# A fused decoder layer: order of instructions at the step from self- to cross-attention, and of the split of the output weights

## What is computed

```python
x = layernorm(x + self_attention(x))            # 32 heads of 16, causal
x = layernorm(x + cross_attention(x, context))  # 32 query heads of 128, 8 key/value heads, rotary positions
x = layernorm(x + experts(x))                   # 16 experts, 4 a token, and a shared one

# cross_attention
q = rope(x @ wq); k = rope(context @ wk); v = context @ wv
w = softmax(where(mask, q @ k.T / sqrt(128), -1e9))    # 4 query heads share a key head
out = (w @ v) @ wo
```

## Time and profile before

| | before |
|---|---|
| median of 3 runs | 1813.35 us (1811.98 to 1816.03) |
| profiled execution, its time | 1817.68 us |
| its span in the profile | 1815.9 us |
| TensorE busy | 1716.0 us (94%) |
| DVE busy | 1332.3 us (73%) |
| ScalarE busy | 925.3 us (51%) |
| GpSimd busy | 895.6 us (49%) |
| granted TensorE clock, mean | 0.978 of 2.4 GHz |

### The profile page before, as it was taken

The page is one execution under the profiler, slowest core; times in us unless marked ns, Lnnn a source line. Parts: engine busy times, 40 slices in busy tenths (PEclk is TensorE's granted clock), DMA queues, the critical chain, the costliest instruction groups (busy, mean ns, idle before and its releaser), DMA issues. The chain is left out here.

```text
span 1815.9 us, 39047 instructions
## 1 busy us (share of the span) xinstructions
PE 1716.0 (94%) x15412; PEld 991.1 (55%) x15412; DVE 1332.3 (73%) x2260; ACT 925.3 (51%) x1548; POOL 895.6 (49%) x732
## 2 busy tenths in 40 slices
PE   6999999899999999999999999999898999999990
PEld 4767676555555555555555555555454555455550
DVE  5788789688888888888888888888888444344445
ACT  4565657665646464556455555556631333333335
POOL 6643022564646454646455555556442455455551
PEclk9999999899999999999999999999999999999995
DMA  9610020211413222214122131212135678787668
GB/s 249 173 45 23 8 62 3 94 65 42 140 42 117 69 78 92 89 51 136 63 78 92 38 105 59 72 69 71 65 124 164 157 151 217 199 223 155 116 105 295
DMA packets 84946, 190.41 MB, mean 105 GB/s; under 512 B 10848, under 2 KB 29664, under 8 KB 82720
## 3 DMA queue, kind: packets, MB, share of 16 engines
q1 hardware_dynamic: 61680, 129.55, 21.2%
q0 software_dynamic: 23088, 58.37, 15.9%
HBM read 124.68 MB, written 63.21 MB: 103 GB/s over the span
## 5 line engine op out<-in xcount | busy, mean ns | idle before, releaser
L288 PE MATMUL bank<-xhl,front_h 128*128 128x512 f16 x704 | 267.5, 380 | 15.1 <-DVEq L68 13.5
L289 PE MATMUL bank<-xhl,front_h 128*128 128x512 f16 x704 | 267.6, 380 | 0.0
L290 PE MATMUL bank<-xhl,front_l 128*128 128x512 f16 x704 | 267.5, 380 | 0.0
L1004 POOL TENSOR_TENSOR xa_xs<-xa_xs,sn 128x512 f32<-128x512 f32 x160 | 233.9, 1462 | 45.7 <-ACT xa_xs L1056 45.7
L1015 POOL TENSOR_TENSOR xa_sc<-xa_sc,xa_rs 128x1024 f32<-128x1024 f32 x32 | 62.3, 1946 | 376.4 <-DVE xa_rs L1255 376.4
L1009 POOL TENSOR_TENSOR xa_rr<-xa_x,xa_xs 128x512 f32<-128x512 f32 x160 | 231.9, 1449 | 12.7 <-DVE xa_x L1160 0.2
L288 PE MATMUL bank<-out_h,xa_oh 128*128 128x512 f16 x512 | 194.9, 381 | 8.8 <-DVE xa_ol L1142 6.7
L1903 POOL DMA_INDIRECT scratch_y<-raw_front,moe_to x79 | 125.2, 1585 | 150.6 <-DVE mo_zl L1956 109.1
L289 PE MATMUL bank<-out_l,xa_oh 128*128 128x512 f16 x512 | 194.7, 380 | 0.0
L290 PE MATMUL bank<-out_h,xa_ol 128*128 128x512 f16 x512 | 194.6, 380 | 0.0
L1055 ACT ACTIVATE xa_xs<-bank 64x512 f32<-64x512 f32 x160 | 95.3, 595 | 131.2 <-PE bank L290 127.6
(11 more groups left out here) (299 smaller groups left out, 4756.5 us busy)
## 6 DMA issues: line engine op xcount, KB each, us to landing
xa_rawc<-in_ew SPq DMA_DIRECT2D x32, 768.0 KB, 5.6
moe_ring<-scratch_w SPq DMA_DIRECT2D x16, 1536.0 KB, 8.8
scratch_w<-xa_chunk_h SPq DMA_DIRECT2D x32, 384.0 KB, 2.3
scratch_w<-xa_chunk_l SPq DMA_DIRECT2D x32, 384.0 KB, 3.3
raw_front<-in_xwq SPq DMA_DIRECT2D x8, 1024.0 KB, 7.7
raw_out<-in_xwo SPq DMA_DIRECT2D x8, 1024.0 KB, 5.4
scratch_y<-xa_zero SPq DMA_DIRECT2D x18, 256.0 KB, 5.9
acc<-in_x POOLq DMA_DIRECT2D x4, 1024.0 KB, 12.9
```

What stands on the lines that cost most here:

```text
L288: pe.matmul(out_ap, ah, bh, start=start and m == 0, stop=False)
L289: pe.matmul(out_ap, ah, bl, start=False, stop=False)
L290: mm = pe.matmul(out_ap, al, bh, start=False, stop=stop and m == n - 1)
L1004: PO.mark(pool.tensor_tensor(xr, xr, sn[:, :].rearrange("p (a s) -> p a s", a=1) .to_broadcast([P, QT // S, S]), ALU.mult), f"sm{r}", st)
```

## The change

1. Self-attention, last group and quarter: DVE makes sums 0 and 1 behind sb3, not behind mx2, and counts them on a semaphore of their own (`s_late`); TensorE turns p2 and p3 ahead of rows 0 and 1.
2. Cross-attention, step (0, 0): TensorE makes the keys r0 of step (0, 1) between s0 and s1, into bank 1; r1 of (0, 1) goes to bank 6, and r3 of (0, 1) waits for cm0, which frees bank 1.
3. Step (0, 0): the four high halves of the tokens of quarter 1 stand ahead of h4 on ScalarE; two low halves ahead of l4 and two behind it on DVE, instead of behind sb1.
4. In all steps q = 1: woh stands behind pe1 on ScalarE, wol behind pl1 on DVE.

```diff
@@ -70,7 +70,7 @@
         for n in (name, *also):
-            key = n if step.i is None else (step.q, n)
+            key = n if step.i is None or isinstance(n, tuple) else (step.q, n)
             assert order[self.cursor] == key, (order[self.cursor], key)
@@ -330,6 +330,7 @@
                 s_st = [sem(f"sa_first{h}") for h in range(2)]
+                s_late = sem("sa_late_sums")
                 s_acc = [sem(f"sa_rows{n}") for n in range(NQ)]
@@ -631,10 +632,15 @@

-                    def most(st, j):
+                    def late_add(st, t):
+                        dve.wait_ge(PE.sem, PE.value(f"w{t}", st))
+                        row = acc[:, t + TQ * (st.q - 1), :]
+                        dve.scalar_tensor_tensor(row, home[f"w{t}"][:, :], 1 / (WS * WS), row, ALU.mult, ALU.add).then_inc(s_late, 1)
+
+                    def most(st, j, also=()):
                         dve.wait_ge(PE.sem, PE.value(f"s{j}", st))
                         DV.mark(dve.tensor_reduce(mx[:, j, :], SB[j % 2][:, :].rearrange("p (a c) -> p a c", c=S), AX.X, ALU.max),
-                                f"mx{j}", st)
+                                f"mx{j}", st, also)

@@ -679,12 +685,18 @@
                             ln.guess(dve, 0)
-                        most(st, 2)
-                        back_add(st, 0)
-                        back_add(st, 1)
+                        late = last and q == 3
+                        most(st, 2, ("w0", "w1") if late else ())
+                        if not late:
+                            back_add(st, 0)
+                            back_add(st, 1)
                         below_most(st, 2)
...
                         below_most(st, 3)
+                        if late:
+                            dve.wait_ge(s_acc[q - 1], 16)
+                            late_add(st, 0)
+                            late_add(st, 1)
                         back_add(st, 2)
@@ -833,10 +845,10 @@
                     back_p(done, (0, 1))
+                    back_p(done, (2, 3))
                     for t in range(2):
-                        pe.wait_ge(DV.sem, DV.value(f"w{t}", done, 1))
+                        pe.wait_ge(s_late, t + 1)
                         ln.turn(pe, 0, t, home[f"w{t}"], rows_h, rows_l)
-                    back_p(done, (2, 3))
                     back_pv(done, 0)
@@ -883,15 +895,16 @@

-                    return bank[4] if r == 1 and isinstance(st.i, int) and (st.i, st.q) == (0, 0) else home[f"r{r}"]
+                    special = {(0, 0, 1): bank[4], (0, 1, 0): bank[1], (0, 1, 1): bank[6]}
+                    return special.get((st.i, st.q, r), home[f"r{r}"])
                 AC = Timeline(sem("xa_act"), events(["r0", "r1", "h0", "r2", "pe0", "pe1", "h1", "r3", "h2", "r4", "hi0", "hi1",
                                                      "h3", "hi2", "hi3", "vh", "h4", "ex0", "ex1", "ch"],
-                                                    [(3, "h4", ["wfh"]), (1, "r1", ["woh"])]), NG,
+                                                    [(3, "h4", ["wfh"]), (1, "pe1", ["woh"])]), NG,
                               ["pe0", "pe1", "hi0", "hi1", "hi2", "hi3"])
...
                                                      "mn0", "mn1", "mx0", "sb0", "mx1", "sb1", "w2", "sum", "rc", "w3", "cl"],
-                                                    [(3, "w0", ["wfl"]), (1, "l0", ["wol"])]), NG,
+                                                    [(3, "w0", ["wfl"]), (1, "pl1", ["wol"])]), NG,
                               ["pl0", "pl1", "lo0", "lo1", "lo2", "lo3", "w0", "w1", "w2", "w3"])
@@ -1066,14 +1079,14 @@
                         copies(st, 1)
+                        rotated_hi(st, 0)
+                        copies(st, 2, ("pe0", "pe1") if alone else ())
+                        if not alone:
+                            back_p(st)
                         if q == 1:
...
                             AC.mark(act.activation(wo_h[:, :, :], raw_o[:, :, :], ACT.Copy, scale=WS), "woh", st)
-                        rotated_hi(st, 0)
-                        copies(st, 2, ("pe0", "pe1") if alone else ())
-                        if not alone:
-                            back_p(st)
                         rotated_hi(st, 1)
@@ -1088,8 +1101,11 @@
                                                ACT.Copy, scale=1 / WS), "vh", st)
+                        if alone:
+                            for t in range(TQ):
+                                ln.high(act, 1, t, bank[4 + t])
                         rotated_hi(st, 4)
-                        if first and q < 3:
+                        if first and 0 < q < 3:
                             for t in range(TQ):
@@ -1193,15 +1209,15 @@
                         rotated_lo(st, 0)
+                        cosine(st, 2, ("pl0", "pl1") if alone else ())
+                        if not alone:
+                            back_p_lo(st)
                         if q == 1:
...
                                                              ALU.mult, ALU.subtract), "wol", st)
-                        cosine(st, 2, ("pl0", "pl1") if alone else ())
-                        if not alone:
-                            back_p_lo(st)
                         rotated_lo(st, 1)
@@ -1224,7 +1240,13 @@
                                 "vl", st)
+                        if alone:
+                            for t in (0, 1):
+                                ln.low(dve, 1, t, bank[4 + t])
                         rotated_lo(st, 4, ("w0", "w1") if alone else ())
+                        if alone:
+                            for t in (2, 3):
+                                ln.low(dve, 1, t, bank[4 + t])
                         if not alone:
@@ -1339,14 +1361,18 @@
                         skipped = {2: ("pt0", "pt1"), 4: ("pv0", "pv1", "pv2", "pv3")} if alone else {}
-                        for r in range(1 if alone else 0, NR):
+                        second = first and q == 1
+                        for r in range(1 if alone or second else 0, NR):
                             if r == 1 and alone:
...
                                 back_p(st)
-                            gbank(pe, f"r{r}", st)
+                            if second and r == 3:
+                                pe.wait_ge(DV.sem, DV.value("cm0", st))
+                            elif not (second and r < 3):
+                                gbank(pe, f"r{r}", st)
                             o = home_of(r, st)
@@ -1376,7 +1402,12 @@
                         scores(st, 0)
-                        scores(st, 1, ("w2", "w3") if alone else ())
+                        if alone:
+                            pe.wait_ge(DV.sem, DV.value("cm3", st))
+                            c, tok = GQ * HD2, slice(QT, 2 * QT)
+                            three_pass(pe, home_of(0, Step(0, 1))[:, :], [(wf_h[:, k, c:c + P], wf_l[:, k, c:c + P], ch[:, k, tok], cl[:, k, tok])
+                                                                         for k in range(KD)])
+                        scores(st, 1, ("w2", "w3", (1, "r0")) if alone else ())
                         if not alone:
```

## The result

The changed kernel is slower by 0.18%: the ratio to the kernel before is 1.0018, with a 95% interval of 1.001 to 1.0026. The medians of 20 runs each are 1819.32 us (1814.16 to 1822.47) and 1815.53 us (1811.98 to 1820.66). On the basis of the prediction, 1813.35, the ratio gives 1816.6 (1815.2 to 1818.1); 1817.9 was forecast. The profiled execution takes 1818.49, with a span of 1816.7.

The account below looks back on a forecast made before the run. The prediction took cross-attention to be bound by TensorE. Its terms, 0.1 (part 1), 0.2 (the seam) and 4.2 (steps q = 1 of groups 1 to 7), gave +4.5 us, put onto the median 1813.35: 1817.9 us, range 1809.5 to 1820.5.

Parts of the forecast that it names:

- check e: Sign at the end of self-attention: its first ptl on DVE at 312.7.
- check a: Sign in step (0,1): no TensorE hole before r1, one of 4 us before the transposes.
- check b: Sign in step (0,1): the values (pv) start on TensorE at 363 to 364.
- all that was ahead of xa_ol on DVE still is: Step (0,1): DVE's work ahead of xa_ol stays, wol included; the projection starts at 371.4, 1.5 ahead of 372.95.
- check c: Sign in (0,1): projection at 371 to 372, behind a 3 to 4.5 us hole for xa_ol, clock 0.50 behind it.
- Rival C: Clock stays at 2.4 GHz behind the long hole in (0,1), later steps cost: +2.8, 1816.2 us; chance 0.17.
- B: Rival: the seam gains 3.3 and 1.5, groups 1 to 7 cost 0; 1808.5 us, faster; chance 0.14.
- check d: Sign in the steps q = 1: wait for xa_ol at 1.2 us, l1 some 1.8 long behind wol.
- the seam: The stretch between the two attentions: -1.5 for an earlier projection, +1.7 for the half clock, together +0.2.
- Rival A: l1, right behind wol, goes ahead of sm3: groups 1 to 7 cost 0.0, the rest 0.3; 1813.7 us; chance 0.20.
- D: Rival: the 1.2 us wait before the projection lowers the clock in three of seven steps, 1.7 each; 1823 us; chance 0.05.

Follow-up runs that it names:

- e3: The changed kernel with woh at the start of the steps q = 1, ahead of all copies, wol left behind pl1; 1818.24 us, one run.
- e7: The changed kernel without part 1, woh and wol halves placed where engines wait in the steps q = 1; ratio 0.9966 to the kernel before, 1811.90 us.
- e6: The kernel before with part 3 alone, the token halves ahead of h4; 1814.76 us, one run.
- e4: The changed kernel with wol split in two halves, one behind pl1 and one behind l1, woh left behind pe1; 1816.15 us, one run.
- e1: The kernel before with part 4 alone, woh behind pe1 and wol behind pl1; ratio 1.004 to the kernel before, 1822.15 us.
- e8: The changed kernel without part 4, woh and wol at their old places, in five rounds; ratio 0.9986 to the kernel before, 1815.74 us.
- e9: e7 without part 2, the next keys staying behind s1; ratio 0.9965 to the kernel before, 1813.22 us.
- e2: The same kernel as e8, the changed kernel without part 4, in three rounds; ratio 1.000 to the kernel before.

## Why the prediction was right

**Part 1** was priced at +0.1 and measures 0.12: the values of self-attention begin 8.31 to 8.32 from P in the profiles with it, 8.17 to 8.19 in those without. The first ptl is at 310.84, in the time of before 312.75 (check e, 312.7).

**Parts 2 and 3.** r1 follows s1 without a hole, and TensorE waits 4.19 for the norm (4.1 expected), from then at half clock (check a). What the prediction did not separate is that part 3 does this alone. The term that was mis-sized: transposes, r3 and r4 were given 6.1, or 7.8 at half clock, and took 8.5. The half clock behind the hole lasted from 354.55 to 359.2, 4.7 us, not 3.4, and cost 2.4, not 1.7. So the values began at 363.03, in the time of before 364.94, when 362.8 to 364.1 was expected (check b, 363 to 364, missed by 0.9).

**Part 4 in (0,1).** The step "all that was ahead of xa_ol on DVE still is" held to a tenth: the projection was expected 1.5 ahead of 372.95 and is 1.56 ahead (check c). The hole before it is 2.4, not the 3 to 4.5 of check c, because TensorE came to it later. The choice that mattered, whether the clock falls behind it, came out as forecast, with 1.66 lost (1.7 in the sum). That is partly luck: the reason given was a hole as long as those of 2.87 and 3.70 behind which it had fallen, and the hole was shorter than both, of a length behind which the clock has fallen in some profiles here and not in others. The prediction also has wol behind woh and held up by ra2 there, without saying which of the two counts; by e3, 0.9 of the projection's place hangs on the wait for woh. Rival C falls with the half clock, and B too: xa_ol of (0,1) is done at 369.4, in the time of before 371.3, when B needed 370. B's own mechanism exists, though: in e7, where the hole is down to 1.8, the clock stays.
The Trainium skill ("TensorE: Matmul & The Clock Gate", section "What's actually happening") has the half clock as the default that activity releases; after agrees, with 0.50 behind both of its long holes, and e6, with 1.00 behind one of 2.65, shows that it need not come to that.

**The steps q = 1.** Priced at 0.6 each from one row, they measure 0.54: 3.8, where 4.2 was expected. The chain came as worked out: wol 2.29, l1 held until sm3's turn was over and ended 0.53 after it (check d: l1 1.8 expected, 1.75 measured). At this step the profile of after is 1.28 early (1.91, less the seam's 0.09 and the 0.54 of step (1,1)), so l1 ends at 615.67 in the time of before, where 615.7 was worked out; l2 then takes 0.68, not 0.75, and that is most of what is missing to 0.6. Rival A, l1 first, is refuted by all seven (l1 1.75 or 1.76 long in each), and e3 and e4 show that here neither woh's wait nor the move as such is the cause, but who has asked when l1 comes. D, a clock that falls in the steps, did not happen: the window from 383 to 1290 stays at 1.00.
The Trainium skill ("SBUF — State Buffer", section "SBUF: two separate sides") has the loser of the lock fully blocked; read, as the prediction did, as l1's whole 0.75 behind the release, it would have made the steps 0.8 each. The lock is in the rows, that length is not: they say 0.53 after the release, and 0.54 a step.

**The sum.** +4.5 was forecast; the traces add up to +3.9 (0.1 to (0,2), 3.8 behind it), the runs say +3.3 (1.8 to 4.7), which is clear of no change, though the prediction held that only some 3.6 could be told from it. What stays open is how much of the seam's result is chance: the two halved stretches need not last as long in each execution.

## What to carry to other kernels

A move that keeps the same instructions ahead of a late result cannot make it earlier: it chooses where the wait is seen. To gain, put the work where its engine idles, in pieces that fit the gap (e7), not behind the instruction that seems to wait. And before an instruction with both operands in SBUF is moved on DVE, look at what GpSimd asks for at that time: a long instruction gives GpSimd the time to ask first, and the short one queued behind it pays. And see what the moved instruction will itself wait for: in (0,1) a wait of 1.0 for woh put the projection 0.9 later and left a hole long enough for the clock to fall.

## What the hardware showed that was not expected

The half clock behind one and the same hole differs from execution to execution. At the end of self-attention the hole for ptl is alike in all kernels here (2.4 to 2.6), but the next output projection, that of the last quarter, begins 15.9 to 16.2 from P in seven of eleven profiles and 17.1 to 17.7 in four (e1, e3, e8, e9). In after the window behind it is back at 1.00, in e1 it is still at 0.50 (after first, then e1):

```profile
318.50:321.50 3.00, 3.00 (x17) 1.46 (x16) 1.33 (x2) 2.57 (x4) 0.00 (x0) 1.00 0.00 0
```

```profile
318.50:321.50 3.00, 3.00 (x24) 2.66 (x23) 2.47 (x5) 0.14 (x1) 0.00 (x0) 0.50 0.00 0
```

That is up to 1.6 us at one hole, as much as a part of this change is worth, so a single profile cannot price such a part. It is not the only place: P itself lies between 305.12 and 311.90 in the eleven profiles (306.70 and 310.61 in e2 and e8, which are one kernel), and what follows the first keys of (7,3) takes 555.2 to 557.8. In e8 (0,2) begins at 78.63 from P, only 0.80 ahead of before, and 1.58 of its gain is hidden in this way (17.63 for 16.05); in e9 likewise 1.0. And the length of a hole does not decide alone: e6's of 2.65 left the clock at 1.00, where the one of 2.87 in before and the one of 2.18 in after have 0.50 behind them. What tells these apart was not tried. Of the holes at the seam in these profiles, by the idle time in their rows, those of up to 1.6 all left it at 1.00 and those of 3.7 and more all brought it down; between them, at 2.0 to 2.9, both were seen.
